# Issuing the skewed read of a key side one step later, behind a head's load, on the queue of a relative-position attention

## The chip, the cores and the metric

The kernel runs on one core of one Trainium2 chip. The metric is device time in microseconds (us) of that core, and before the change it was 1897.5 us as the median of three runs (1889.75 to 1898.95). One further execution was taken by the hardware profiler, and all rows below are from it. The core has a matrix engine (PE, with its weight loads as PEld), a vector engine (DVE), a scalar engine (ACT), a general engine (POOL), a sync engine (SP) whose queue issues all DMAs of this kernel, and 16 DMA engines that move the data.

## The reference, cut to what matters

The program is two transformer layers on `x` of 8 x 512 x 128. Only the first attention is touched by the change. It has 16 heads of width 8 for each of the 8 batches, so 128 heads, and each head's scores are 512 x 512:

```python
scores  = einsum('bhqd,bhkd->bhqk', Q, K) * scale
c2p     = einsum('bhqd,shd->bhqs', Q, pos_key) * scale      # s: 128 relative positions
c2p     = take_along_axis(c2p, clip(rel + 64, 0, 127))      # rel = k - q
p2c     = einsum('bhkd,shd->bhks', K, pos_query) * scale
p2c     = swapaxes(take_along_axis(p2c, clip(-rel + 64, 0, 127)), -1, -2)
probs   = softmax(scores + c2p + p2c)
ctx     = einsum('bhqk,bhkd->bhqd', probs, V)
```

After it come a residual and a layer norm, a gated feed-forward, a second attention with another relative shift, another layer norm and a feed-forward of four wide products. They are not changed.

## The kernel before, in words

Each engine has a program of its own, and engines meet at semaphores. The first attention (`attention(0)`, where `rel` is true) walks over the 128 heads, one head a step. Heads 0 to 3 are written out, then a loop runs 14 times over 8 steps, then 12 steps are written out again. A step n on PE turns and weighs the probabilities of older heads, scores tiles of 128 queries six tiles ahead, and makes two small products for heads further ahead:

- `key_side` (L736 to L741), for head n+7: the key side of the relative positions. DVE copies it to a tile `keyside` (`key_out`, L751 to L755).
- `correction` (L743 to L750), for head n+5, at the end of the step. It first transposes a tile `sheared` (L748) and adds the query side to it (L749). ACT copies the sum to `corr` (`corr_out`, L757 to L761).

The gather of the reference is made by skewed DMAs through DRAM. `shear_a_write` (L631) writes `keyside` of a head to the buffer `shear_a`; `shear_a_read` (L636) reads it back with a row pitch that is one element longer, so that each row is shifted by one, into `sheared`. `shear_b_write` (L642) and `shear_b_read` (L648) do the same with `corr`, and the result, `band`, is added to the scores by DVE (L946). The buffers `shear_a`, `keyside` and `sheared` have four places, taken in turn.

All of these DMAs are issued by SP in the order in which its program has them (`sync_step`, L675). `hold` (L595) makes SP wait for a semaphore; while it waits, nothing behind it is issued. In step n SP writes the key side of head n+6, loads the stack of head n+8 (`head_load`, two DMAs, L608 and L609), writes the correction of head n+4, reads the band of head n+3, and reads the sheared key side of head n+6, for which it waits until the write of the same step has landed. In every fourth step it also loads tables and offsets (L621, L628, L629) and stores a group of four finished heads (`group_store`, L671, with the load of the next values, L673). That store waits for `group_out` of ACT (L1057), which copies the weighed sums to `outs` at the end of ACT's step. Before the first step SP's opening part does the first such moves (L252 to L298). In the last eight steps `sync_tail` of the next stage (L1230) puts its own DMAs between the steps.

PE waits for the sheared tile at the head of `correction`, and its instructions run in order:

```python
pe.wait_ge(sheared_in[h.slot % 4], BASE + 16 * (h.use(4) + 1))
```

Of the kernel before, what the change touches and what calls it, by code (L numbers as in the profile page):

```python
# [50 lines left out]
CORR_AHEAD, KEY_AHEAD, LOAD_AHEAD = 5, 7, 8  # L51
# [13 lines left out]
def build(nc, t):  # L65

    top = ExitStack()
    with top:
# [66 lines left out]
        def opening(att):  # L135
# [23 lines left out]
            full, left = work.pair("full", [C, 2, T]), work.pair("left", [C, 2, T])  # L159
# [38 lines left out]
            def program(block):  # L198

                @block.sync  # L200
                def _(sp):
# [86 lines left out]
                    att.shear_b_read(sp, 0)  # L288
                    att.shear_a_read(sp, 4)
                    att.shear_b_write(sp, 2)  # L290
                    att.shear_a_read(sp, 5)
                    att.shear_b_read(sp, 1)
                    att.shear_b_write(sp, 3)
                    att.offset_load(sp, GROUP)
# [204 lines left out]
        def attention(layer):  # L499
# [95 lines left out]
            def hold(q, event, value):  # L595

                q.wait_ge(event, BASE + value)
                q.sem_inc(held_off, 1)
# [3 lines left out]
            def head_load(sp, h):  # L602

                j, b = h.slot, h.n // H
                own = bass.ts(h.n % H, DH)
                if rel:
                    rows = stack[0][b, :, own].rearrange("a c j t -> (c j) a t")
                    sp.dma_start(stk[j][0:SR, KS:QLO + 1, :], rows).then_inc(stk_in[j], 16)  # L608
                    sp.dma_start(stk[j][0:SR, QHI, :], rows[:, 1, :]).then_inc(stk_in[j], 16)  # L609
                else:  # L610
                    src = stack[1][b, own].rearrange("c j w -> (c j) w")
                    spins = src[:, 3 * T:5 * T + 2].rearrange("r (a t) -> r a t", a=2)[:, :, 0:T]
                    sp.dma_start(stk[j][0:SR, KEY:NEAR + 1, :].rearrange("r a t -> r (a t)"), src[:, 0:3 * T]).then_inc(stk_in[j], 16)
                    sp.dma_start(stk[j][0:SR, FAR, :], src[:, 2 * T:3 * T]).then_inc(stk_in[j], 16)
                    sp.dma_start(stk[j][SR:R1, EDGE, :], src[:, T + 1:2 * T + 1]).then_inc(stk_in[j], 16)
                    sp.dma_start(stk[j][SR:R1, NEAR:FAR + 1, :], spins).then_inc(stk_in[j], 16)

            def tab_load(sp, h):

                src = table[bass.ds(h.n % H, GROUP)].rearrange("h r c -> r h c")  # L620
                sp.dma_start(tabs[0:SR, h.slot:h.slot + GROUP, :], src).then_inc(tab_in[h.slot // GROUP], 16)  # L621

            def offset_load(sp, h):

                src, own = offsets[h.n // H, bass.ds(h.n % H, GROUP)], slice(h.slot, h.slot + GROUP)
                event = offset_in[h.slot // GROUP]
                for arr in (QLO, QHI):
                    sp.dma_start(stks[RA:RB, own, arr, :], src[:, arr - QLO].rearrange("h k t -> k h t")).then_inc(event, 16)  # L628
                sp.dma_start(stks[RB:RS, own, KS, :], src[:, 2:4].rearrange("h a k t -> (a k) h t")).then_inc(event, 16)  # L629

            def shear_a_write(sp, h):  # L631

                hold(sp, key_copied, h.n + 1)
                sp.dma_start(shear_a[h.slot % 4, :, SPAN:SPAN + T], keyside[h.slot % 4][:, :]).then_inc(a_written[h.slot % 4], 16)

            def shear_a_read(sp, h):  # L636

                hold(sp, a_written[h.slot % 4], 16 * (h.use(4) + 1))
                skew = bass.AP(shear_a.tensor, (h.slot % 4) * 128 * PITCH_A, [[PITCH_A + 1, 128], [1, T]])
                sp.dma_start(sheared[h.slot % 4][:, :], skew).then_inc(sheared_in[h.slot % 4], 16)  # L640

            def shear_b_write(sp, h):  # L642

                hold(sp, corr_copied, h.n + 1)
                dst = shear_b[h.slot % 4, :, REL:PITCH_B].rearrange("p (n c) -> p n c", n=NT)[:, :, 0:REL]
                sp.dma_start(dst, corr[h.slot % 2][:, :, :]).then_inc(b_written[h.slot % 4], 16)

            def shear_b_read(sp, h):  # L648

                hold(sp, b_written[h.slot % 4], 16 * (h.use(4) + 1))  # L650
                skew = bass.AP(shear_b.tensor, (h.slot % 4) * 128 * PITCH_B + REL, [[PITCH_B - 1, 128], [1, NT * wide]])
                sp.dma_start(band[h.slot % bands][:, :, :].rearrange("p n c -> p (n c)"), skew).then_inc(band_in[h.slot % bands], 16)

            def edge_write(sp, h):

                hold(sp, corr_copied, h.n + 1)
                dst = shear_e[h.slot % E_RING].rearrange("(n p) c -> p n c", p=128)[:, :, REL:2 * REL]
                sp.dma_start(dst, corr[h.slot % corrs][:, :, :]).then_inc(e_written[h.slot % corrs], 16)

            def edge_read(sp, h):  # L660

                hold(sp, e_written[h.slot % corrs], 16 * (h.use(corrs) + 1))
                skew = bass.AP(shear_e.tensor, (h.slot % E_RING) * T * PITCH_E + REL,
                               [[PITCH_E - 1, 128], [128 * PITCH_E, NT], [1, REL]])
                sp.dma_start(band[h.slot % bands][:, :, :], skew).then_inc(band_in[h.slot % bands], 16)

            def group_store(sp, h, more):

                g = h.use(GROUP)
                hold(sp, out_copied, g + 1)  # L670
                sp.dma_start(heads_out[bass.ts(g, GROUP)], outs[:, :]).then_inc(out_written, 16)  # L671
                if more:
                    sp.dma_start(vs[h.slot // GROUP][:, 0:GROUP * NT * VC], values[g + vslots]).then_inc(v_in[h.slot // GROUP], 16)  # L673

            def sync_step(sp, i, j, left, weighed=True):  # L675

                n = unroll * i + j
                if rel:
                    if left >= CORR_AHEAD + 1:
                        shear_a_write(sp, Head(i, j + CORR_AHEAD + 1))  # L680
                    if left >= LOAD_AHEAD:
                        hold(sp, score_mm, 4 * (n + 1))
                        head_load(sp, Head(i, j + LOAD_AHEAD))
                    if left >= CORR_AHEAD - 1:
                        hold(sp, added, 4 * (n + 1))
                        shear_b_write(sp, Head(i, j + CORR_AHEAD - 1))
                    if left >= CORR_AHEAD - 2:
                        shear_b_read(sp, Head(i, j + CORR_AHEAD - 2))
                    if j % GROUP == GROUP - 1 and left >= LOAD_AHEAD + GROUP:
                        tab_load(sp, Head(i, j + LOAD_AHEAD + 1))  # L690
                    if j % GROUP == GROUP - 1 and left >= LOAD_AHEAD:
                        offset_load(sp, Head(i, j + LOAD_AHEAD + 1 - GROUP))
                    if left >= CORR_AHEAD + 1:
                        shear_a_read(sp, Head(i, j + CORR_AHEAD + 1))
                else:
                    if left >= CORR_AHEAD:
                        edge_write(sp, Head(i, j + CORR_AHEAD))
                    if weighed and left >= CORR_AHEAD - 1 or 0 < j < FIRST and not weighed:
                        if weighed:
                            hold(sp, added, 4 * (n + CORR_AHEAD - bands))  # L700
                        edge_read(sp, Head(i, j + CORR_AHEAD - 1))
                    if left >= LOAD_AHEAD:
                        if not isinstance(i, int) or n + LOAD_AHEAD >= unroll:
                            hold(sp, maxed, 4 * (n + LOAD_AHEAD - unroll + 1))
                        head_load(sp, Head(i, j + LOAD_AHEAD))
                if weighed and j % GROUP == GROUP - 1:
                    group_store(sp, Head(i, j + 1 - 2 * GROUP), left >= GROUP * (vslots - 1))
# [1414 lines left out]
```

## Time and profile before

| | us |
|---|---|
| median of 3 runs | 1897.5 |
| lowest and highest | 1889.75, 1898.95 |
| profiled execution | 1880.74 |
| its span | 1879.0 |
| PE busy in the span | 1699.8 (90%) |
| DVE busy | 1468.3 (78%) |
| ACT busy | 1448.4 (77%) |
| DMA, 16 engines, mean share of q1 | 69.3% |

The span is what the profile covers from the first to the last instruction; the profiled execution's own time is 1.7 us longer. The opening and the first attention take some 810 us of it. PE's clock is told as a share of 2.4 GHz: 1.00 or 0.50.

### The profile page before, as it was taken

Reading aid. Unit: us, or ns where it says so; the run is one execution under the profiler, and the core shown is the slowest. Engines: PE = TensorE matmul, PEld = TensorE weight load, DVE = VectorE, ACT = ScalarE, POOL = GpSimd, SP = SyncE. Lnnn points to the kernel's source line nnn. Section 1 sums busy time; section 2 is a strip of 40 time slices with the busy share of each in tenths; the row PEclk is TensorE's granted clock in tenths of the full one; section 3 lists DMA queues with packets and bytes.
Section 4 is the critical chain, followed back from the end, with each engine's and each line's share of the span. In section 5 each row is a group of like instructions: output and inputs, shape, how many; then the busy total and the mean of one; then the engine's idle time right before and its main releaser. Section 6 shows DMA issues by size and latency. Waiting matters only on the chain.

```text
span 1879.0 us, 44062 instructions
## 1 busy us (share of the span) xinstructions
PE 1699.8 (90%) x11694; PEld 1033.3 (55%) x11694; DVE 1468.3 (78%) x3533; ACT 1448.4 (77%) x2573; POOL 80.2 (4%) x102
## 2 busy tenths in 40 slices
PE   5369999999999999878758999999999989999998
PEld 2146666666666666545535666666666544455453
DVE  5659999999999999859887999999999873443332
ACT  4449999998999999859888999999999972322222
POOL 0000000000000000015410000000000000000000
PEclk9669999999999999989879999999999999999999
DMA  6778999998999999766998777777777751010000
GB/s 195 273 245 274 300 292 307 298 297 278 288 289 295 297 287 301 234 190 231 344 333 241 220 221 217 223 219 217 222 221 213 224 155 40 28 39 22 22 6 12
DMA packets 414360, 404.45 MB, mean 215 GB/s; under 512 B 36969, under 2 KB 334561, under 8 KB 414177
## 3 DMA queue, kind: packets, MB, share of 16 engines
q1 hardware_dynamic: 414305, 403.80, 69.3%
q8 instruction: 24, 0.39, 0.1%
q14 instruction: 31, 0.25, 0.0%
HBM read 226.89 MB, written 176.30 MB: 215 GB/s over the span
## 4 chain that ended last, share of the span: by engine, by line
PE 54%; DMA 14%; SPq 9%; issue 7%; DVE 7%; ACT 6%; DVEq 0%; POOL 0%; ACTq 0%; POOLq 0%
PE bank L842 15%; PE bank L1934 12%; PE bank L855 8%; DMA a_band<-shear_e 5%; PE bank L821 5%; DMA shear_a<-a_keyside 4%; PE bank L748 3%; DMA a_sheared<-shear_a 2%; DVE a_negmax L954 2%; PE bank L823 2%; ACT a_probt L1051 2%; PE bank L1926 1%; PE bank L1927 1%; PE bank L827 1%; PE bank L1955 1%
## 5 line engine op out<-in xcount | busy, mean ns | idle before, releaser
L1044 ACT ACTIVATE a_prob<-bank,a_negmax 128x512 f32<-128x512 f32 x1024 | 702.6, 741 | 27.4 <-DVE a_negmax L954 25.8
L954 DVE TENSOR_REDUCE a_negmax<-bank 128x1 f32<-128x512 f32 x1024 | 695.1, 679 | 0.2 <-issue 0.2
L1051 ACT COPY a_probt<-bank 128x512 f32<-128x512 f32 x1024 | 599.4, 633 | 28.0 <-PE bank L842 23.5
L842 PE MATMUL bank<-ident,a_prob 128*128 128x128 f32 x4096 | 602.6, 281 | 13.1 <-ACT a_probt L1051 9.7
L842 PEld LDWEIGHTS bank<-ident,a_prob 128*128 128x128 f32 x4096 | 446.4, 142 | 170.9 <-ACT a_probt L1051 117.3
L946 DVE TENSOR_TENSOR bank<-bank,a_band 128x128 f32<-128x128 f32 (+3 forms) x1024 | 339.1, 343 | 71.9 <-DMA a_band<-shear_e 24.4
L821 PE MATMUL bank<-a_stks 74*128 74x192 bf16 (+7 forms) x1024 | 324.7, 317 | 29.7 <-ACT a_prob L1044 26.0
L855 PE MATMUL bank<-a_probt,a_vs 128*32 128x512 f32 x2048 | 274.8, 611 | 0.8 <-ACT a_probt L1051 0.4
L823 PE MATMUL bank<-a_stks 74*128 74x320 bf16 (+5 forms) x768 | 201.3, 262 | 0.0
L821 PEld LDWEIGHTS bank<-a_stks 74*128 74x128 bf16 (+1 forms) x1024 | 100.5, 98 | 163.8 <-ACT a_prob L1044 143.6
L934 DVE COPY_PREDICATED bank<-a_mask,bank 128x128 f32<-128x128 uint32 (+1 forms) x512 | 140.2, 274 | 20.1 <-PE bank L827 18.6
L748 PE MATMUL bank<-ident,a_sheared 128*128 128x128 f32 x512 | 110.3, 293 | 33.2 <-DMA a_sheared<-shear_a 25.8
L2000 DVE TENSOR_TENSOR d_drop<-bank,d_s 128x128 f32<-128x128 f32 x32 | 7.1, 283 | 170.4 <-PE bank L1955 170.4
L827 PE MATMUL bank<-a_stks 74*128 74x128 bf16 (+1 forms) x512 | 112.0, 219 | 6.2 <-DVE bank L934 5.8
L761 ACT COPY a_corr<-bank 128x512 f32<-128x512 f32 x128 | 76.2, 595 | 51.8 <-PE bank L749 38.6
L1934 PE MATMUL bank<-d_ha,d_h1T 128*128 128x512 f32 x256 | 112.3, 592 | 0.0
L1934 PE MATMUL bank<-d_hb,d_h2T 128*128 128x512 f32 x256 | 111.2, 592 | 0.0
L755 DVE COPY a_keyside<-bank 128x512 f32<-128x512 f32 x128 | 86.7, 678 | 19.8 <-PE bank L741 19.8
L748 PEld LDWEIGHTS bank<-ident,a_sheared 128*128 128x128 f32 x512 | 74.8, 146 | 46.5 <-issue 25.1
L749 PE MATMUL bank<-a_tabs,a_stks 65*128 65x128 bf16 x512 | 98.6, 226 | 0.0
L1985 ACT ACTIVATE d_hb<-bank,d_fs 128x512 f32<-128x512 f32 x32 | 22.0, 688 | 90.6 <-PE bank L1934 90.6
L827 PEld LDWEIGHTS bank<-a_stks 74*128 74x128 bf16 x512 | 49.3, 96 | 73.3 <-DVE bank L934 47.9
(179 smaller groups left out, 1597.5 us busy)
## 6 DMA issues: line engine op xcount, KB each, us to landing
a_band<-shear_b SPq DMA_DIRECT2D x128, 512.0 KB, 5.2
shear_a<-a_keyside SPq DMA_DIRECT2D x128, 256.0 KB, 4.1
a_sheared<-shear_a SPq DMA_DIRECT2D x128, 256.0 KB, 4.1
shear_b<-a_corr SPq DMA_DIRECT2D x128, 256.0 KB, 3.4
shear_e<-a_corr SPq DMA_DIRECT2D x128, 256.0 KB, 2.3
a_band<-shear_e SPq DMA_DIRECT2D x128, 256.0 KB, 3.3
a_stks<-stack SPq DMA_DIRECT2D x256, 96.0 KB, 2.5
a_stks<-stack SPq DMA_DIRECT2D x384, 48.0 KB, 2.4
```

The lines of the kernel that those rows point to most:

```text
L748: pe.matmul(corr_bank[:, q], sheared[h.slot % 4][:, q], ident[:, :], is_transpose=True, start=True, stop=False)
L821: last = pe.matmul(score[:, 0:c], k[:, qlo, q], k[:, keys, 0:c], start=True, stop=True)
L823: last = pe.matmul(score[:, c:T], k[:, qhi, q], k[:, keys, c:T], start=True, stop=True)
L827: last = pe.matmul(other[:, 0:e - a], k[:, qhi, q], k[:, keys, a:e], start=True, stop=True)
L842: last = pe.transpose(turned_bank[k][:, n * 128:(n + 1) * 128], prob[h.slot % 2][:, n, k * 128:(k + 1) * 128], ident[:, :])
L855: part = pe.matmul(cbank[32 * j:32 * j + VW, cols], vs[g][:, at:at + VW], probt[h.slot + j][:, k, cols], start=(k == 0), stop=(k == NT - 1 ...
L934: v.copy_predicated(score[:, a:e], mask[:, 0:e - a], other[:, 0:e - a]).then_inc(fixed, 1)
L946: v.tensor_tensor(score[:, a:e], score[:, a:e], band[h.slot % bands][:, n, w:w + e - a], ALU.add).then_inc(added, 1)
L954: v.tensor_reduce(negmax[h.slot % 2][:, n:n + 1], score[:, :], AX.X, ALU.max, negate=True).then_inc(maxed, 1)
L1044: nc.scalar.activation(prob[h.slot % 2][:, n, :], score[:, :], ACT.Exp, bias=negmax[h.slot % 2][:, n:n + 1]).then_inc(exped, 1)
L1051: nc.scalar.copy(probt[h.slot][:, k, :], turned_bank[k][:, :]).then_inc(copied, 1)
L1934: last = pe.matmul(dst[:, :], w[:, k, 128 * m:128 * m + 128], src[:, k, :], start=(k == 0), stop=(k == KH - 1))
```

## The change

In `sync_step` the read of the sheared key side leaves the end of the step. It now stands behind `head_load`, one step later: step n reads head n+5, whose key side was written in step n-1, where it read head n+6, written in the same step. The opening does one read less (head 5), and step 0 does it.

```diff
@@ -288,7 +288,6 @@
                     att.shear_b_read(sp, 0)
                     att.shear_a_read(sp, 4)
                     att.shear_b_write(sp, 2)
-                    att.shear_a_read(sp, 5)
                     att.shear_b_read(sp, 1)
@@ -681,6 +680,8 @@
                     if left >= LOAD_AHEAD:
                         hold(sp, score_mm, 4 * (n + 1))
                         head_load(sp, Head(i, j + LOAD_AHEAD))
+                    if left >= CORR_AHEAD:
+                        shear_a_read(sp, Head(i, j + CORR_AHEAD))
                     if left >= CORR_AHEAD - 1:
                         hold(sp, added, 4 * (n + 1))
                         shear_b_write(sp, Head(i, j + CORR_AHEAD - 1))
@@ -690,8 +691,6 @@
                     if j % GROUP == GROUP - 1 and left >= LOAD_AHEAD:
                         offset_load(sp, Head(i, j + LOAD_AHEAD + 1 - GROUP))
-                    if left >= CORR_AHEAD + 1:
-                        shear_a_read(sp, Head(i, j + CORR_AHEAD + 1))
```

`CORR_AHEAD` is 5, `LOAD_AHEAD` is 8. What moves is shown by the order of SP's instructions. A number behind a tile's name is its buffer: 77 to 80 are the four places of `sheared`, 73 to 76 those of `keyside`. REGISTER_ALU and ISA are the address arithmetic of the loop.

First the place where a group of heads is stored, from SP in the loop, before; `a_sheared_78` is the tile of the head whose key side was written in the same step:

```order
L640 DMA a_sheared_78<-shear_a 128x512 [waits a0_a_written1]
L597 REGISTER_ALU
L671 ISA [waits a0_out_copied]
L671 DMA heads_out<-a_outs 128x512
L673 ISA
L673 DMA a_vs_61<-values 128x144
L597 REGISTER_ALU
L634 DMA shear_a<-a_keyside_75 128x512 [waits a0_key_copied]
L597 ISA
L608 ISA [waits a0_score_mm]
L608 DMA a_stks<-stack 48x2x512
L609 ISA
```

The same place after the change (all line numbers from L597 on are one lower):

```order
L670 ISA [waits a0_out_copied]
L670 DMA heads_out<-a_outs 128x512
L672 ISA
L672 DMA a_vs_61<-values 128x144
L596 REGISTER_ALU
L633 DMA shear_a<-a_keyside_75 128x512 [waits a0_key_copied]
L596 ISA
L607 ISA [waits a0_score_mm]
L607 DMA a_stks<-stack 48x2x512
L608 ISA
L608 DMA a_stks<-stack 48x512
L639 DMA a_sheared_78<-shear_a 128x512 [waits a0_a_written1]
```

The read into `a_sheared_78` stood ahead of the group's store; it now stands behind the store, the load of values, the next key side's write and two loads.

Then the end of the stage, from SP in the written-out steps, before; `m_sums` and `m_wo` belong to the next stage:

```order
L640 DMA a_sheared_79<-shear_a 128x512 [waits a0_a_written2]
L86 ISA x47
L1189 DMA m_sums<-heads_out 128x1x64 [waits a0_out_written]
L1189 DMA m_sums<-heads_out 128x1x64 x6
L634 DMA shear_a<-a_keyside_76 128x512 [waits a0_key_copied]
L646 DMA shear_b<-a_corr_67 128x4x128 [waits a0_added,a0_corr_copied]
L652 DMA a_band_68<-shear_b 128x1024 [waits a0_b_written0]
L640 DMA a_sheared_80<-shear_a 128x512 [waits a0_a_written3]
L1239 DMA m_wo<-in_WoT 128x128
```

And after the change:

```order
L86 ISA x47
L1188 DMA m_sums<-heads_out 128x1x64 [waits a0_out_written]
L1188 DMA m_sums<-heads_out 128x1x64 x6
L633 DMA shear_a<-a_keyside_76 128x512 [waits a0_key_copied]
L639 DMA a_sheared_79<-shear_a 128x512 [waits a0_a_written2]
L645 DMA shear_b<-a_corr_67 128x4x128 [waits a0_added,a0_corr_copied]
L651 DMA a_band_68<-shear_b 128x1024 [waits a0_b_written0]
L1238 DMA m_wo<-in_WoT 128x128
L1238 DMA m_bo<-in_bo 128x128
```

The reads of the last two heads moved behind the next stage's semaphore resets (the 47 of L86) and its seven loads of sums, and the last one (`a_sheared_80`) also behind five loads of weights that follow.

## Rows read from the trace of the kernel before

**Rows 1.** Busy time by stretch of the first attention, all engines.

```profile
core 0: us, PE busy (x) PEld busy (x) DVE busy (x) ACT busy (x) POOL busy (x), PEclk, DMA share, GB/s
128.00:785.00 657.00, 640.56 (x5346) 415.17 (x5344) 624.42 (x1592) 617.66 (x1128) 0.10 (x1) 1.00 0.92 289
```

**Rows 2.** Waits of SP's queue, 120 to 795 us: total, times, longest.

```profile
SPq L598 <- DMA shear_a<-a_keyside: 87.3, 80, 3.8
```

**Rows 3.** Waits of the engines, same stretch.

```profile
PE bank L748 <- DMA a_sheared<-shear_a: 11.2, 9, 4.1
```

**Rows 4.** SP's issues around one group store: start, duration, operation.

```profile
639.36 0.35 SPq L640 DMA_DIRECT2D a_sheared<-shear_a  x1
640.83 0.38 SPq L671 DMA_DIRECT2D heads_out<-a_outs  x1
...
641.94 0.33 SPq L634 DMA_DIRECT2D shear_a<-a_keyside  x1
642.78 0.34 SPq L608 DMA_DIRECT2D a_stks<-stack  x1
...
643.85 0.39 SPq L646 DMA_DIRECT2D shear_b<-a_corr  x1
```

**Rows 5.** ACT's group copy there, and in the next group.

```profile
639.96 0.61 ACT L1057 COPY a_outs<-bank 128x512 f32<-128x512 f32 x1
...
660.91 0.60 ACT L1057 COPY a_outs<-bank 128x512 f32<-128x512 f32 x1
```

**Rows 6.** First transpose of three corrections on PE (heads 100, 101, 105).

```profile
639.24 0.32 PE L748 MATMUL bank<-ident,a_sheared 128*128 128x128 f32 x1
...
644.48 0.30 PE L748 MATMUL bank<-ident,a_sheared 128*128 128x128 f32 x1
...
665.77 0.32 PE L748 MATMUL bank<-ident,a_sheared 128*128 128x128 f32 x1
```

**Rows 7.** The stores of groups, 165 to 770 us.

```profile
L671 SPq DMA_DIRECT2D heads_out<-a_outs x29: 372/383/387, 167.5 to 768.9; - x29
```

**Rows 8.** Issue to landing of the write L646 at 643.85.

```profile
DMA to landing us min/median/max: 2.4/2.4/2.4
```

**Rows 9.** Issue to landing of all 128 reads of `a_sheared`.

```profile
DMA to landing us min/median/max: 2.7/4.1/7.0
```

**Rows 10.** Chain of waits, from the landing to PE at 432.83: start, us, what.

```profile
432.69 0.14 issue
```

**Rows 11.** DVE's copy of head 101's key side.

```profile
632.42 0.68 DVE L755 COPY a_keyside<-bank 128x512 f32<-128x512 f32 x1
```

**Rows 12.** PE after waits for the sheared tile, first transposes of corrections.

```profile
432.83 0.30 PE L748 MATMUL bank<-ident,a_sheared 128*128 128x128 f32 x1 [1.57 <-DMA a_sheared<-shear_a]
...
439.43 0.30 PE L748 MATMUL bank<-ident,a_sheared 128*128 128x128 f32 x1
...
694.20 0.30 PE L748 MATMUL bank<-ident,a_sheared 128*128 128x128 f32 x1 [2.19 <-DMA a_sheared<-shear_a]
...
787.46 0.45 PE L748 MATMUL bank<-ident,a_sheared 128*128 128x128 f32 x1 [4.14 <-DMA a_sheared<-shear_a]
```

**Rows 13.** Stretches after those three waits, columns as in rows 1.

```profile
432.90:439.40 6.50, 6.50 (x44) 4.10 (x44) 4.54 (x12) 4.33 (x8) 0.00 (x0) 0.74 0.71 198
...
694.30:700.00 5.70, 5.70 (x52) 3.86 (x53) 5.07 (x14) 4.75 (x9) 0.00 (x0) 1.00 0.68 199
785.50:792.20 6.70, 4.74 (x25) 3.31 (x29) 4.86 (x13) 2.18 (x4) 0.00 (x0) 0.50 0.84 238
```

**Rows 14.** SP's issues at the end of the stage.

```profile
776.16 4.56 SPq L1189 DMA_DIRECT2D m_sums<-heads_out  x7
780.85 0.50 SPq L634 DMA_DIRECT2D shear_a<-a_keyside  x1
...
783.15 0.32 SPq L640 DMA_DIRECT2D a_sheared<-shear_a  x1
```

**Rows 15.** PE's correction of head 126.

```profile
777.74 0.33 PE L748 MATMUL bank<-ident,a_sheared 128*128 128x128 f32 x1
```

## Prediction

> **What bounds the kernel now.** I read the busy times by stretch first. From 128 to 785 us, inside the first attention, PE is busy 640.56 of 657 us at the full clock, so all its idle time there is 16.4 us, spread over some 125 heads; DVE (624) and ACT (618) are close behind, and the DMA engines are busy 92% of it [rows 1]. A head costs PE 5.24 us, from one correction to the next [rows 6]. So PE's own instructions bound the stage, DMAs run close beside it, and whatever stops PE adds to the time in full, since no engine has room to make it up.
>
> Then I read the waits, SP's queue and the engines apart. SP waits 80 times, 87.3 us in total, for the write of `shear_a` to land [rows 2]; this is the wait that the change takes away. But SP isn't the bound. What the stage pays for late sheared tiles is what PE waits for them: 9 times, 11.2 us, the longest 4.1 us, which is head 127 at the very end [rows 3, 12]. The other eight are 7.1 us together.
>
> Last I read the queue's order in time against PE's order, because the change moves one instruction past others in SP's queue. At a group store SP issues the read of head 101 at 639.36, then waits for ACT's copy of the group, which ends at 640.57 (639.96 and 0.61), stores at 640.83, loads values, writes the next key side at 641.94, issues two loads and reaches the next instruction at 643.85 [rows 4, 5]. PE begins the correction of head 101 at 644.48 [rows 6]. Before the change the read had 5.12 us for its way. This place decides the case.
>
> **The change part by part.**
>
> Removed: the wait of SP between a write and the read behind it. Hidden until now, worth at most what PE idles. I take back 9 us: the 7.1 us of PE waits outside the tail, and some 1.4 us of a half clock that one of them brought (below), with a little of the rest. The ends are 7 and 16 us (all of PE's idle time in the stretch).
>
> Moved, in the steps without a store: the read of head m is now issued behind the write of head m+1 and two loads. The write can go 0.1 us after DVE's copy of that key side; from the write to the instruction behind the loads are 1.91 us (641.94 to 643.85) [rows 4]. The copy of head 101 ends at 633.10 [rows 11], so the read of head 100 would be issued at 635.1, and its correction starts at 639.24 [rows 6]: 4.1 us for a median way of 4.1 us [rows 9]. That looks tight, but the median holds the reads that were issued right behind a band read of 512 KB. Now the last band read lies most of a step back, with 400 KB between, and I take 3.3 us, between the shortest (2.7) and the median. So these reads land about 0.8 us early, and only slow ones (the longest took 7.0) stop PE. I take +4 us for the stage, with 0 and 25 as ends. Behind it in SP's queue, the write of `shear_b` and the read of the band now come about 0.5 us later than their neighbours let them behind a store, and earlier elsewhere, since SP no longer waits: nothing.
>
> Moved, at a store: the read of a head now stands behind the store, and the store waits for ACT. The read takes the place that L646 has now, 3.28 us after the end of ACT's copy (640.57 to 643.85) [rows 4, 5]. None of this can shrink: ACT's copy needs PE's last weighing of the step, and the rest is SP's own time for five issues and their addresses. PE reaches the correction 3.91 us after the end of ACT's copy in this group and 4.26 in the next (661.51 to 665.77) [rows 5, 6], 4.08 as a mean. So the read has 0.8 us for its way, and it needs at least 2.7 us [rows 9]. The way is new, so I bound it. A write of the same 256 KB from this very place took 2.4 us [rows 8]; the shortest read took 2.7 and the median 4.1 [rows 9]. The ring is nearly empty here, because SP stood still for ACT, and so I take 3.0. With 0.14 us from the landing to PE [rows 10], PE stops for 3.28 + 3.0 + 0.14 - 4.08 = 2.34 us. By 2.7 it would be 2.04, by 4.1 it would be 3.44. There are 29 such stores with a read behind them [rows 7], at heads 13, 17 and so on to 125: 29 x 2.34 = 68 us (59 and 100 at the ends). Nothing hides it, since PE is busy all the time around it; so the whole of it counts.
>
> The Trainium skill has a rule on the way of a DMA (DMA: Bandwidth & Descriptors, Anatomy of one DMA): about 2.0 us fixed and bytes over 436 GB/s. By it 256 KB take 2.6 us, an estimate, and the sum of the stalls would be 56 us. The shortest read here, 2.7 us, agrees.
>
> The clock: waits of PE can halve it. Of the three longest waits for a sheared tile, 1.57, 2.19 and 4.14 us, the stretches behind show 0.74, 1.00 and 0.50 [rows 12, 13]. After the first of them the next correction came 6.60 us later (432.83 to 439.43) and not 5.24: 1.4 us lost. New waits of 2.3 us lie between a case that halved the clock and one that didn't, so I take 6 in 10: 29 x 0.6 x 1.4 = 24 us, with 0 and 41 (each of them) as ends.
>
> The tail: the reads of heads 126 and 127 move behind the next stage's DMAs. In the rows the seven loads of sums run from 776.16 to 780.72, and the write of the last key side is at 780.85 [rows 14]. The read of head 126 is issued before them now. It would be at 781.3 or a little earlier, while PE wants it at 777.74 [rows 15]: its correction slips to about 784. The correction of head 127 is late already (787.46) [rows 12], and it would come one step of 5.2 us behind head 126, or when its own read lands, which five loads push by some 2 to 3 us: 789 to 791. Net +2 us, 0 and +5 as ends. The opening only loses one read, of head 5, which isn't wanted soon: nothing.
>
> The sum: 68 + 24 + 4 + 2 - 9 = +89 us, made against the profiled execution, 1880.7 to about 1970. That execution is 16.8 us below the median of the runs, 1897.5, and I put the same difference on the median: 1986 us, 4.7% slower.
>
> **The rivals.**
>
> Faster. SP's wait of 87.3 us is the real brake: with it gone, all of SP's issues move forward, the group's store too, and the sheared tile is always there. For it speaks that the chain of waits ran through these DMAs wherever PE stopped. It would win the 16.4 us of PE's idle time, 1881 us. The point from which it decides is whether the read behind a store leaves before 641.2, 3.3 us ahead of PE; but it cannot leave before ACT's copy ends at 640.57 and SP has issued five others. Chance 0.03.
>
> No change: the stall at the store is real, but the three steps behind it run faster by what it costs, because SP, DVE and ACT are ahead then. Against it: PE is 97.5% busy [rows 1]. Time 1897. Chance 0.02.
>
> Every read late. The three reads between two stores share the ring with the write and the loads issued just ahead of them, so they need 4.5 us and not 3.3, while they have 4.1. Then 87 more waits of some 0.6 us, +52 us: 2038. For it speaks the 92% of the DMA engines; against it that the slower pace gives them air, and that bytes and order within a step hardly change. Chance 0.15.
>
> The clock falls at every stop and stays down longer. The Trainium skill describes this (TensorE: Matmul & The Clock Gate, HAM oscillation): a loop whose PE waits for a DMA each turn is slowed each turn. As a mechanism of this kernel: 29 times 1.4 us and, where it stays down for twice as long as behind 432.83, as it did behind 787.46, twice that. Instead of 24 us the clock costs 41 to 81, and the time is 2003 to 2043. The wait of 2.19 us with a clock of 1.00 behind it speaks against it. Chance 0.18.
>
> **How the numbers follow.** The forecast itself has 0.62. Its own range is 1945 (shortest way, no fall of the clock, 16 us won: 59 + 2 - 16 = +45) to 2035 (100 + 41 + 4 + 2 - 9 = +138). The last two rivals reach above that, so the range for 8 in 10 goes from 1948 to 2042. About 0.5% is what a measurement of this kernel can tell from no change. All cases but the first two are slower by far more: faster 0.03, same 0.02, slower 0.95.
>
> **What would show it.** SP's waits for the write of `shear_a` vanish, and its waits for ACT's `a_outs` grow. PE's waits at L747 for the sheared tile go from 9 to about 29 or more and from 11 us to 60 to 100, every fourth head, each about 2 to 3.5 us. Behind a store the read of `a_sheared` leaves about 3.3 us after ACT's copy. PE's clock shows halves between 130 and 785 us. If the steps without a store also stop PE, the third rival holds. I am wrong if the corrections behind a store start without a wait, or if the read there lands in under 1 us.

## The result, and the profile after

The changed kernel takes 1999.4 us as the median of four runs (1989.89 to 2004.15), against 1893.6 us for the kernel before over the four runs made of it by then: ratio 1.0543, 95% interval 1.0504 to 1.0582. The profiled execution took 1989.89 us, with a span of 1988.1 us, 109.1 us more than before.

The busy time by stretch of the changed kernel, columns as in [rows 1]; the third row is a stretch behind one of PE's new waits:

```profile
core 0: us, PE busy (x) PEld busy (x) DVE busy (x) ACT busy (x) POOL busy (x), PEclk, DMA share, GB/s
128.00:890.00 762.00, 681.24 (x5322) 437.77 (x5321) 625.98 (x1586) 617.02 (x1122) 0.10 (x1) 0.93 0.82 251
...
727.30:730.70 3.40, 3.40 (x19) 1.46 (x16) 3.14 (x8) 2.87 (x6) 0.00 (x0) 0.50 0.97 329
```

Two things differ from [rows 1]. PE is idle 81 us of the stretch (762 less 681) and was 16. And its busy time has grown by 41 us for the same matmuls, while the mean clock fell from 1.00 to 0.93, that is, PE ran parts of the stretch at 1.2 instead of 2.4 GHz (called a half clock below). DVE and ACT do the same work in the same time.

The waits of the engines and of SP's queue in the changed kernel, 120 to 895 us (what waits, for what: total, times, longest):

```profile
PE bank L747 <- DMA a_sheared<-shear_a: 77.3, 37, 5.5
...
SPq L597 <- DVE a_keyside L754: 109.2, 62, 4.2
SPq L597 <- ACT a_corr L760: 61.6, 62, 1.8
SPq L597 <- ACT a_outs L1056: 51.8, 29, 2.9
```

SP's wait for the write of `shear_a`, 87.3 us in [rows 2], is gone. In its place SP waits for the engines. The last row is the one that matters: 29 waits for ACT's group copy, one at each group store. PE's waits for the sheared tile went from 11.2 us [rows 3] to 77.3. One of them, in time: SP's issues, ACT's group copy and PE's corrections of heads 100 to 102:

```profile
720.16 0.38 SPq L670 DMA_DIRECT2D heads_out<-a_outs  x1
720.73 0.36 SPq L672 DMA_DIRECT2D a_vs<-values  x1
721.28 0.33 SPq L633 DMA_DIRECT2D shear_a<-a_keyside  x1
722.13 0.34 SPq L607 DMA_DIRECT2D a_stks<-stack  x1
722.65 0.34 SPq L608 DMA_DIRECT2D a_stks<-stack  x1
723.10 0.35 SPq L639 DMA_DIRECT2D a_sheared<-shear_a  x1
```

```profile
719.31 0.60 ACT L1056 COPY a_outs<-bank 128x512 f32<-128x512 f32 x1
```

```profile
718.58 0.32 PE L747 MATMUL bank<-ident,a_sheared 128*128 128x128 f32 x1
...
726.04 0.30 PE L747 MATMUL bank<-ident,a_sheared 128*128 128x128 f32 x1 [2.10 <-DMA a_sheared<-shear_a]
...
732.65 0.30 PE L747 MATMUL bank<-ident,a_sheared 128*128 128x128 f32 x1
```

ACT's copy ends at 719.91, SP reaches the read at 723.10, 3.19 us later, and PE starts at 726.04, after 2.10 us of waiting. Before, the same three corrections stood 5.24 us [rows 6] and 5.35 us apart. Here they are 7.46 and 6.61 us apart: the first gap holds the wait, the second the half clock. The wait repeats at heads 13, 17 and so on to 125: 29 waits of 1.57 to 2.64 us, 69.4 us in all, one of them at each group store. The half clock follows 22 of them.

### The profile page after: what moved, and what is told of

Read it like the earlier page. It is cut to its first block, busy times and chain, and to the rows that moved or that the text cites. A ratio compares the mean times of both kernels' runs of the same rounds, so it can differ in the third digit from the quotient of the medians.

```text
span 1988.1 us, 44062 instructions
## 1 busy us (share of the span) xinstructions
PE 1744.7 (88%) x11694; PEld 1058.1 (53%) x11694; DVE 1472.9 (74%) x3533; ACT 1450.5 (73%) x2573; POOL 80.1 (4%) x102
## 4 chain that ended last, share of the span: by engine, by line
PE 44%; DMA 14%; SPq 13%; ACT 10%; issue 9%; DVE 8%; DVEq 0%; POOL 0%; ACTq 0%; POOLq 0%
PE bank L1933 11%; PE bank L841 11%; DMA a_band<-shear_e 6%; PE bank L854 6%; DMA a_sheared<-shear_a 6%; PE bank L820 4%; ACT a_probt L1050 3%; PE bank L747 3%; ACT a_prob L1043 3%; DVE a_negmax L953 3%; PE bank L1925 1%; PE bank L1926 1%; PE bank L822 1%; PE bank L1954 1%; DVE bank L945 1%
## 5 line engine op out<-in xcount | busy, mean ns | idle before, releaser
L841 PE MATMUL bank<-ident,a_prob 128*128 128x128 f32 x4096 | 620.2, 286 | 13.4 <-ACT a_probt L1050 11.2
L841 PEld LDWEIGHTS bank<-ident,a_prob 128*128 128x128 f32 x4096 | 460.4, 146 | 184.1 <-ACT a_probt L1050 106.4
L820 PE MATMUL bank<-a_stks 74*128 74x192 bf16 (+7 forms) x1024 | 334.4, 327 | 32.0 <-ACT a_prob L1043 28.1
L854 PE MATMUL bank<-a_probt,a_vs 128*32 128x512 f32 x2048 | 283.9, 629 | 0.8 <-ACT a_probt L1050 0.4
L747 PE MATMUL bank<-ident,a_sheared 128*128 128x128 f32 x512 | 117.5, 307 | 97.8 <-DMA a_sheared<-shear_a 92.4
L748 PE MATMUL bank<-a_tabs,a_stks 65*128 65x128 bf16 x512 | 105.4, 236 | 0.0
L754 DVE COPY a_keyside<-bank 128x512 f32<-128x512 f32 x128 | 87.3, 682 | 20.9 <-PE bank L740 20.9
```

The lines of the kernel that those rows point to most:

```text
L747: pe.matmul(corr_bank[:, q], sheared[h.slot % 4][:, q], ident[:, :], is_transpose=True, start=True, stop=False)
L820: last = pe.matmul(score[:, 0:c], k[:, qlo, q], k[:, keys, 0:c], start=True, stop=True)
L841: last = pe.transpose(turned_bank[k][:, n * 128:(n + 1) * 128], prob[h.slot % 2][:, n, k * 128:(k + 1) * 128], ident[:, :])
L854: part = pe.matmul(cbank[32 * j:32 * j + VW, cols], vs[g][:, at:at + VW], probt[h.slot + j][:, k, cols], start=(k == 0), stop=(k == NT - 1 ...
```

## The experiments

The times of before were taken on the same chip as each run: 1893.3 us for the first four kernels, 1899.4 for the next four, 1891.7 for the last two.

**Only the store passed.** `e1_swap` is the kernel before, with the read moved from ahead of the group store to behind it, and nothing else:

```diff
-                    if left >= CORR_AHEAD + 1:
-                        shear_a_read(sp, Head(i, j + CORR_AHEAD + 1))
...
                 if weighed and j % GROUP == GROUP - 1:
                     group_store(sp, Head(i, j + 1 - 2 * GROUP), left >= GROUP * (vslots - 1))
+                if rel and left >= CORR_AHEAD + 1:
+                    shear_a_read(sp, Head(i, j + CORR_AHEAD + 1))
```

> The kernel before, with one exchange: the read of the sheared key side stays at the end of its step but stands behind the group store instead of ahead of it. Nothing is deferred past the next key side's write or the next load. My theory (what costs is how long after ACT's group copy SP reaches the read): the read would leave 1.4 us after the end of the copy instead of 3.3, so PE waits some 0.4 to 0.7 us at 29 places, too short to halve the clock: 1900 to 1915 us. Rival A (passing the store at all puts the read late by the full amount): about 2000. Rival B (the store doesn't matter, being behind the next write and loads in the ring does): 1893, as before.

Measured: 1919.8 us, ratio 1.0153 (1.0114 to 1.0192). Better than rival A, worse than my range. The waits at the store were small, as expected: 14 of them, 6.8 us. But the next head waited too, 25 times, 25.0 us in all (9.3 us in the kernel before):

```profile
668.73 0.30 PE L748 MATMUL bank<-ident,a_sheared 128*128 128x128 f32 x1 [0.45 <-DMA a_sheared<-shear_a]
...
675.18 0.30 PE L748 MATMUL bank<-ident,a_sheared 128*128 128x128 f32 x1 [1.02 <-DMA a_sheared<-shear_a]
```

That is what I had left out. The next head's read isn't issued later for PE than before (4.8 us ahead of the point where PE wants it, in the median, against 4.65), but its way, from issue to landing, is longer: 5.5 us against 4.3. Both stand right behind a band read; why the way grew isn't shown. SP waits 87.3 us for the writes in this kernel too.

**The store behind the next read.** `e2_store_late` is the changed kernel; at every fourth step the next step's moves are pulled ahead of the store:

```diff
+            def early_moves(sp, i, j, left):
+                n = unroll * i + j
+                if left >= CORR_AHEAD + 1:
+                    shear_a_write(sp, Head(i, j + CORR_AHEAD + 1))
+                if left >= LOAD_AHEAD:
+                    hold(sp, score_mm, 4 * (n + 1))
+                    head_load(sp, Head(i, j + LOAD_AHEAD))
+                if left >= CORR_AHEAD:
+                    shear_a_read(sp, Head(i, j + CORR_AHEAD))
...
+                    if j % GROUP or not weighed:
+                        early_moves(sp, i, j, left)
...
+                if rel and j % GROUP == GROUP - 1:
+                    early_moves(sp, i, j + 1, left - 1)
                 if weighed and j % GROUP == GROUP - 1:
                     group_store(sp, Head(i, j + 1 - 2 * GROUP), left >= GROUP * (vslots - 1))
```

> The changed kernel, but at every fourth step the next step's key side write, head load and read are issued ahead of the group store, not behind it. The read is still a step past its write and still behind the write and the load, in every step. My theory: the 29 waits of 2.4 us vanish, the clock stays at 1.00 between 130 and 785 us, and with SP's waits for the write gone as well the time is 1880 to 1900. Rival B (a read behind the write and the loads in the ring is late by itself): the waits stay, now in all steps, 1950 or more.

Measured: 1905.8 us, 1.0072 (1.0043 to 1.0102), a little above my range. The loss of 106 us shrinks to 12 by the order around the store alone. The waits of PE and the clock from 140 to 780 us:

```profile
PE bank L755 <- DMA a_sheared<-shear_a: 23.1, 25, 1.8
...
140.00:780.00 640.00, 610.93 (x5085) 395.57 (x5089) 596.18 (x1507) 584.75 (x1070) 0.00 (x0) 0.99 0.92 285
```

The waits at the head behind the store are gone (3 of 0.5 us in all). The 23.1 us are of the head after it, whose read now took 4.8 us in the median, while PE wanted it 4.0 us after its issue.

**The wait without the idle engine.** `e3_fill` keeps the changed kernel and fills PE's wait with work:

```diff
                         pe.wait_ge(copied, BASE + 4 * own.n + 3)
+                        if weighed and j % GROUP == 0:
+                            for _ in range(FILL):           # FILL = 9
+                                pe.matmul(corr_bank[:, :], stk[(j + CORR_AHEAD) % unroll][0:RF, QLO, 0:128],
+                                          stk[(j + CORR_AHEAD) % unroll][0:RF, KS, :], start=True, stop=True)
                         correction(pe, Head(i, j + CORR_AHEAD))
```

> The changed kernel, with nine extra matmuls of 512 columns ahead of the correction in each step behind a group store. They write a bank that the correction overwrites, and their result isn't used. At the full clock they take some 2 us, inside the 2.4 us that PE waits there. My theory (of the 106 us, some 45 are the halved clock): the landing and so the wait's end don't move, but the clock stays at 1.00: 1950 to 1965 us. Rival C (the halved clock is beside the point, since the time is set by the DMAs and SP): 1995 to 2005, or above it by what the matmuls overrun.

Measured: 1960.6 us, 1.0356 (1.0319 to 1.0392), as expected. Its row from 140 to 780 us, and below it that of the changed kernel:

```profile
140.00:780.00 640.00, 613.86 (x4929) 383.53 (x4928) 550.99 (x1389) 538.89 (x987) 0.00 (x0) 1.00 0.85 262
```

```profile
140.00:780.00 640.00, 575.47 (x4504) 369.02 (x4503) 529.21 (x1336) 521.18 (x948) 0.00 (x0) 0.93 0.82 253
```

The clock is back at 1.00, with some 2 us more work in each of these steps. The step that ends with the wait takes about as long as in the changed kernel (7.81 us as a mean against 7.89, worked out from the starts of the corrections at heads 13 to 121), so the read's landing hardly moved; the step behind it fell from 6.89 to 5.87 us. So keeping the clock up wins some 39 us (1999.4 less 1960.6; on different chips, but the kernel before took 1893.6 and 1893.3 us on them).

That is net. Between the two profiled executions it is 28.0 us (spans of 1988.1 and 1960.1), and in `e3_fill` PE waits 13.9 us for sheared tiles outside the stops and the tail, where the changed kernel waits 2.4: with the half clock PE reaches the next correction later, and the read, whose way is the same (5.1 us), is there in time. So the half clock itself cost that execution of the changed kernel about 40 us.

**A shorter wait.** `e4_before_load` issues the read ahead of the two loads:

```diff
                     if left >= CORR_AHEAD + 1:
                         shear_a_write(sp, Head(i, j + CORR_AHEAD + 1))
+                    if left >= CORR_AHEAD:
+                        shear_a_read(sp, Head(i, j + CORR_AHEAD))
                     if left >= LOAD_AHEAD:
                         hold(sp, score_mm, 4 * (n + 1))
                         head_load(sp, Head(i, j + LOAD_AHEAD))
-                    if left >= CORR_AHEAD:
-                        shear_a_read(sp, Head(i, j + CORR_AHEAD))
```

> The changed kernel, with the read ahead of the head's load and behind the key side's write. At a store the read leaves about 1.1 us sooner, 2.2 us after ACT's copy. My theory: 29 waits of some 1.3 us instead of 2.4 us, and the clock falls rarely: 1925 to 1945 us. If every stop halved the clock whatever its length it would be 1965. Rival B (bytes ahead in the ring set the landing): the wait shrinks by more than 1.1 us, since 144 KB are gone from ahead of it; its way falls from 3.1 us to 2.6.

Measured: 1942.5 us, 1.0261 (1.0226 to 1.0296), in the range. The 29 waits are 33.0 us, 1.14 each, 1.25 less than in the changed kernel for an issue 1.1 us sooner. The way stayed at 3.15 us (3.0 there), so rival B's shorter way isn't seen; and the clock is 0.99 from 140 to 780. But the next head waits too, 1.1 us at 26 places.

**The two halves of the change.** `e7_only_store` defers one read of four in the kernel before, the one at the store, and `e8_others` puts just this one back in the changed kernel:

```diff
 e7_only_store, against the kernel before
+                    if left >= CORR_AHEAD and weighed and j % GROUP == 0:
+                        shear_a_read(sp, Head(i, j + CORR_AHEAD))        # behind head_load
...
-                    if left >= CORR_AHEAD + 1:
+                    if left >= CORR_AHEAD + 1 and j % GROUP != GROUP - 1:
                         shear_a_read(sp, Head(i, j + CORR_AHEAD + 1))    # at the step's end
```

```diff
 e8_others, against the changed kernel
-                    if left >= CORR_AHEAD:
+                    if left >= CORR_AHEAD and (j % GROUP or not weighed):
                         shear_a_read(sp, Head(i, j + CORR_AHEAD))
...
+                    if j % GROUP == GROUP - 1 and left >= CORR_AHEAD + 1:
+                        shear_a_read(sp, Head(i, j + CORR_AHEAD + 1))
```

> The kernel before, with the change made in one step of four only: the read whose place is ahead of a group store is issued behind the store, the next write and the next load. The other three reads stay a few issues behind their own write, with the wait for it. My theory (the cost is all at the stores): 29 waits of 2.4 us and the halved clock as in the changed kernel, 1985 to 2000 us. Rival B (reads issued behind a write and a load are late in every step, by their place in the ring): a quarter of the loss, about 1920.

> The opposite: the changed kernel, with only the read behind a group store put back ahead of it, where the kernel before has it, with its wait. The other three of four are deferred. My theory: no wait at the 29 places and no fall of the clock. From the kernel with the late store I also expect the next read, which has a store, a band read, a write and a load just ahead of it in the ring, to come about 1 us late: 1895 to 1915 us. Rival B: 1970 or more. If the deferral itself were a gain wherever no store is passed: 1880.

Measured: 1994.6 us, 1.0511 (1.0472 to 1.0550), and 1922.2 us, 1.0132 (1.0082 to 1.0181). One deferred read of four makes nearly the whole loss, 95 of 106 us, by the same 29 waits (68.8 us) and nearly the same clock. The waits of PE and the clock in `e7_only_store`:

```profile
PE bank L750 <- DMA a_sheared<-shear_a: 60.2, 27, 2.6
...
140.00:780.00 640.00, 578.33 (x4477) 371.18 (x4476) 527.13 (x1328) 519.94 (x944) 0.00 (x0) 0.92 0.81 250
```

The other three alone cost 23 us, 7 more than I allowed, and the waits are at the head after the store: 28 of them, 33 us (9.3 us before), beside one at the tail. The two halves don't add up to the whole: behind a wait of 2.4 us the next read has time enough.

**Both edits.** `e5_both` is `e2_store_late` with the read ahead of the load in `early_moves`.

> The changed kernel with both edits: the next step's key side write, read and load are issued ahead of the group store, and the read stands ahead of the load. SP never waits for a write of shear_a, and each read has some 5 us for its way instead of 4. The kernel with the late store alone still waited 1.0 us at 29 places, for the read after the one at the store, whose way was 4.8 us with 4.0 available. My theory (what counts is the time left against the way): these waits go too and the time is 1880 to 1890 us, a little under the kernel before. Rival B (the bytes just ahead in the ring lengthen the way by as much as is won): 1900 to 1910, no better than the late store alone.

Measured: 1889.7 us over 12 runs, against 1899.4: 0.9957 (0.9939 to 0.9975), at the upper end of the range in us and 0.4% faster than the kernel before. Reads land in time in all steps but those after a store, where waits of some 0.6 us stay, and PE waits 6.0 us for head 126 at the end. Where the 0.4% come from, the traces don't show: at heads 5 to 124 PE waits 13.4 us for sheared tiles here and 10.3 in the profile of before, which is of an execution 16.8 us below its median.

**The store late in the kernel before.** `e6_before_store_late` pulls only the next write and load ahead of the store, and leaves the read at its old place:

```diff
             def early_moves(sp, i, j, left):
...
                     head_load(sp, Head(i, j + LOAD_AHEAD))
-                if left >= CORR_AHEAD:
-                    shear_a_read(sp, Head(i, j + CORR_AHEAD))
```

> The kernel before, with the group store issued behind the next step's key side write and head load; the read keeps its place behind its own write and the wait for it. It tells whether the store, ahead of the next write, is what made the kernel before late now and then (9 waits, 7 us of them outside the last head). My theory: the writes are no longer held up by ACT's copy, so SP is less behind, and the time is 1883 to 1893 us. Rival: the wait for the write is what holds SP, and nothing changes, 1893.

Measured: 1921.5 us, 1.0132 (1.0097 to 1.0168). Missed, and on the wrong side. SP's wait for the write grew:

```profile
SPq L598 <- DMA shear_a<-a_keyside: 117.2, 82, 3.6
```

It was 87.3 us [rows 2], and PE waits 28 times, 30.3 us, at the head after a store. With SP's pause at the store gone, writes and reads follow more closely on the band reads, their way is longer (the median read took 4.5 us against 4.1), and a queue that waits for each write pays for it. So the wait that the change removes may well matter where DMAs are dense. That, and that the pause at the store hides it in the kernel before, is my reading of these rows; no run takes the pause or the wait away alone.

**The tail, and how near to a band read.** `e9_tail` is `e5_both` with the last two reads as in the kernel before. `e10_read_first` also issues the read ahead of the next key side's write:

```diff
 e9_tail, against e5_both
-                if left >= CORR_AHEAD:
+                if left >= LOAD_AHEAD - 1:
                     shear_a_read(sp, Head(i, j + CORR_AHEAD))
...
+                if rel and left in (CORR_AHEAD + 1, CORR_AHEAD + 2):
+                    shear_a_read(sp, Head(i, j + CORR_AHEAD + 1))
```

> The kernel with both edits (next write, read and load ahead of the group store, the read ahead of the load), and the reads of the last two heads issued ahead of the next stage's DMAs again, as in the kernel before. There PE waited 6.0 us for head 126. My theory: the tail costs 17 to 19 us from the correction of head 125 to that of 127, and 15 us as in the kernel before: some 3 us less than with both edits alone, 1884 to 1890 us. Rival (the tail is paced by the next stage's DMAs anyway): no change in the profile from head 125 to 127.

> The kernel of the tail run, with the read issued ahead of the next key side's write too, so one issue (0.5 to 1 us) sooner, and directly behind the last band read of 512 KB. If only the time left counts, the remaining waits at the head after a store (0.6 us each in the kernel with both edits) go and the time falls by up to 13 us. If the bytes ahead count as much, the way grows to the 6 us seen in the kernel before behind a band read, and the time stays within 5 us.

Measured: 1882.2 us over 10 runs, against 1891.7: 0.9953 (0.9933 to 0.9972), some 2 us below my range and by its ratio not to be told from `e5_both`; and 1918.1 us, 1.0136 (1.0112 to 1.0160). PE's waits for the sheared tile in `e9_tail`, and below it those of PE and SP in `e10_read_first`, 130 to 790 us:

```profile
PE bank L757 <- DMA a_sheared<-shear_a: 9.6, 14, 2.6
```

```profile
PE bank L757 <- DMA a_sheared<-shear_a: 35.4, 37, 2.3
...
SPq L597 <- DMA shear_a<-a_keyside: 106.9, 68, 4.0
```

From the correction of head 125 to that of 127 `e9_tail` takes 13.2 us, the kernel before 14.8 and `e5_both` 19.1. The gain of 6 us over `e5_both` stands in these profiles alone; the medians, of different chips, don't show it. One issue sooner, in `e10_read_first`, the read stands right behind a band read, and SP reaches it before the write that it needs has landed, though that write was issued 3.3 to 6.4 us earlier (medians by kind of step): SP waits for the write again, and the read's way is 6.1 us in half of the steps. So being earlier in the queue is a gain only down to that point. Which of the two, the wait or the longer way, costs more isn't told apart.

## Why the prediction was right, by its steps

Forecast: 1986 us, 89 us slower. Measured: 1999.4 us, 105.8 slower. The mechanism and the place were as predicted; one term, the clock, was too small.

- *The stop at the store.* Predicted: 29 waits of 2.34 us, 68 us. Measured: 29 of 2.39 us, 69.4 us. SP reached the read 3.19 us after ACT's copy in the median (predicted 3.28), and the read's way was 3.0 us in the median there (predicted 3.0, with 2.7 to 4.1 as ends). The rule of the Trainium skill (DMA: Bandwidth & Descriptors, Anatomy of one DMA) gave 2.6 us. That section fits it on DMAs that the general engine issues, and here SP issues them; the trace is 0.4 us above it. That this place makes the loss is shown by `e7_only_store` and `e2_store_late`.
- *The clock.* Predicted 24 us, from 17 falls of 1.4 us each. Measured 39 us net by `e3_fill` and 41 us in the trace of the changed kernel. Between 130 us and the end of the stage it has 113 us at 1.2 GHz in 23 stretches of 3.4 or 6.8 us; the kernel before had one of 3.4 and, at head 127, one of 6.8. Here the last one, of 6.8, belongs to the tail. The other 22 each follow one of the 29 waits, where I had 6 in 10. The step behind a stop, without its own wait, took 5.36 us as a mean where no fall followed (six times), 6.63 us with a fall of 3.4 us (13 times) and 8.04 us with one of 6.8 us (nine times). So a short fall costs 1.3 us, near the 1.4 predicted, and a long one 2.7: 13 x 1.3 and 9 x 2.7 make 41 us. I had taken the price from the one fall in the middle of the stage [rows 12, 13] and left the longer one at its end to a rival. The fourth rival, with 41 to 81 us, was nearer to the clock term than the forecast, though not each stop halved the clock. The total came out close all the same; this term's missing 17 us are the largest part that the forecast had wrong.

```profile
174.40:181.20 6.80, 6.76 (x31) 3.69 (x32) 3.53 (x8) 3.51 (x6) 0.00 (x0) 0.50 0.89 297
455.00:578.00 123.00, 108.21 (x906) 69.99 (x910) 105.13 (x266) 102.95 (x189) 0.00 (x0) 1.00 0.85 264
```

The first of these rows of the changed kernel is a fall of 6.8 us behind head 13's stop, the second holds six stops with no fall.

- *The reads at the other steps.* Predicted +4 us with 0.8 us to spare. Their way was 2.8 to 3.0 us in two of three (predicted 3.3), and outside the stores and the tail PE waited 2.4 us in all (the read behind each stop took 5.2 us, but had 6.1). The third rival is refuted for this kernel. But `e2_store_late` and `e8_others` show that they had this room only because PE stood still at each store: without it the read after a store is late by 0.9 us in the one and 1.2 in the other.
- *What is won back.* Predicted 9 us; PE's waits outside the stops and the tail fell from 10.3 us to 2.4, 8 us.
- *The tail.* Predicted +2 us. Corrections 125 to 127 went from 14.8 to 17.3 us, +2.6, and the place was as predicted: PE waits for head 126, whose read is issued behind the next stage's loads.

```profile
883.32 0.51 SPq L633 DMA_DIRECT2D shear_a<-a_keyside  x1
883.94 0.35 SPq L639 DMA_DIRECT2D a_sheared<-shear_a  x1
```

```profile
887.64 0.45 PE L747 MATMUL bank<-ident,a_sheared 128*128 128x128 f32 x1 [5.54 <-DMA a_sheared<-shear_a]
```

With the sizes of the trace the sum is 69 + 41 - 8 + 3 = 105 us, against 109.1 between the two spans and 105.8 between the medians. The remaining 4 us between the spans these rows don't place.

The prediction's own lower bound is added up wrongly: 1897.5 + 45 is 1942.5 us and not 1945. The measured time lies far above either.

The first rival (SP's wait for the write is the brake) was wrong for the kernel as it was changed, but not empty: `e5_both` and `e9_tail`, which cut SP's wait for the write from 87 us to 13 and 11 and move the read past no store, are 0.4 and 0.5% faster than the kernel before. That this comes of the shorter wait isn't shown, and the wait isn't all that counts: `e2_store_late`, with no such wait at all but the read behind the two loads, is 0.7% slower.

## What to carry to other kernels

When a DMA issue is moved in an in-order queue, list what it is moved past and look for the one that waits for a computing engine: here one such store in four steps made nearly the whole loss, and removing the wait for the write won back at most 8 us. A wait that recurred on the engine that bounds the stage cost its length (69 us) plus what the clock took afterwards (41 us), and filling it with work of no use separated the two. What helped this queue was to move the waiting store back behind the issues that others need soon, with each read one step behind its write but not directly behind the band read.

## What the runs showed of the hardware

- The length of PE's wait alone doesn't decide whether its clock falls. Six waits in a row between 452 and 575 us, of 2.40 to 2.55 us, had no half clock behind them, nor had the one of 1.57 us at head 125; the 22 others, of 2.10 to 2.64 us, had. The waits of 1.1 us in `e4_before_load` left it at 0.99 on average. What else decides it isn't settled by these runs.
- With nine matmuls of 512 columns, 2.1 us together, in each such wait, the clock stayed at 1.00 from 130 us until the tail at 856 us (`e3_fill`).
- The way of the same 256 KB read goes with how far back the last band read of 512 KB was issued. As medians over the steps of one kind: 3.0 us where it was 4.1 us back (changed kernel, heads 16, 20 and so on), 5.2 us at 2.5 us back (there, the heads after a stop), 5.9 at 1.05 (`e4_before_load`) and 6.1 to 6.2 at 0.6 to 0.8 us back (`e10_read_first`). It isn't a law: at 2.5 to 2.6 us there are medians from 3.4 (`e5_both`) to 5.2, and at 0.6 to 0.7 us back from 4.0 (`e7_only_store`) to 6.1. What else it goes with isn't settled.
